# A vision tower on one core: query, key and value products from halves in fp16, and eleven more products of ones at the start

## What is computed

```python
h = embed(x, W, b)                      # patches of 768 numbers to 256
h = concatenate([cls_tok, h])           # 37 tokens per image
# attention on the normalized tokens, 4 heads of 64 channels
q, k, v = (split(norm(h) @ w.T) for w in (Wq, Wk, Wv))
p = softmax(causal(q @ k.T))
A_mem = (elu(q) + 1) @ mem / ((elu(q) + 1) @ z + 1e-6)
out = (g * A_mem + (1 - g) * (p @ v)) @ Wo.T + bo       # g = sigmoid(betas)
h = h + out
# one shared expert and the best 2 of 8 experts, hidden width 1024
h = h + shared(norm(h)) + sum(gate_e * expert_e(norm(h)) for e in top2(norm(h) @ gate_w.T))
```

## Time and profile before

| | |
|---|---|
| median of 3 executions | 331.41 us (331.07 to 331.76) |
| the profiled execution | 331.46 us |
| its span, first to last instruction | 329.6 us |
| busy share of the span | PE 96%, PEld 81%, DVE 67%, ACT 54%, POOL 43% |
| the chain that ended last | PE 77%, DVE 12%, issue 4%, DMA 3% |
| granted clock of TensorE, mean | 0.996 of full speed |

### The profile page before, as it was taken

How to read it: one execution, slowest core, us unless ns; L and a number is a source line. 1 busy time by engine, 2 the same in 40 slices (tenths; PEclk the granted TensorE clock), 3 DMA queues, 4 the chain that set the end, 5 groups by cost and what they waited for, 6 DMA issues and landing times.

```text
span 329.6 us, 9583 instructions
## 1 busy us (share of the span) xinstructions
PE 315.7 (96%) x3378; PEld 268.2 (81%) x3378; DVE 222.0 (67%) x501; ACT 177.3 (54%) x342; POOL 143.3 (43%) x216
## 2 busy tenths in 40 slices
PE   7999999999999899999999999999999999999990
PEld 6788888888888799999998777778777877777870
DVE  0336778888888888899887786855465655555540
ACT  1145667667786788557667877842323232323220
POOL 0566445555645432211451434555444453635131
PEclk9999999999999999999999999999999999999998
DMA  7775334332123113943689775332423232333221
GB/s 237 254 214 201 108 107 165 125 90 57 59 87 93 30 30 77 322 111 75 159 222 304 247 193 162 66 51 50 63 36 59 40 50 51 47 52 39 29 33 17
DMA packets 18641, 36.35 MB, mean 110 GB/s; under 512 B 3331, under 2 KB 10982, under 8 KB 18598
## 3 DMA queue, kind: packets, MB, share of 16 engines
q1 hardware_dynamic: 12166, 27.71, 26.5%
q0 software_dynamic: 6432, 8.03, 16.0%
HBM read 28.52 MB, written 7.21 MB: 108 GB/s over the span
## 4 chain that ended last, share of the span: by engine, by line
PE 77%; DVE 12%; issue 4%; DMA 3%; POOL 1%; ACT 1%; POOLq 1%; SPq 0%; DVEq 0%; ACTq 0%
PE bank L795 20%; PE bank L808 14%; PE bank L481 10%; PE bank L810 6%; PE bank L506 5%; PE bank L618 3%; PE bank L577 3%; PE bank L516 2%; DMA out_rows<-y,add_id 2%; PE bank L529 2%; PE bank L543 2%; PE bank L566 2%; DVE hid_lo L1339 2%; PE bank L436 2%; PE bank L533 1%
## 5 line engine op out<-in xcount | busy, mean ns | idle before, releaser
L795 PEld LDWEIGHTS bank<-x_t,weights 128*128 x1248 | 87.6, 98 | 25.6 <-issue 0.2
L795 PE MATMUL bank<-x_t,weights 128*128 128x128 f16 x1248 | 103.9, 219 | 0.0
L972 ACT ACTIVATE act_out<-bank 128x512 f32<-128x512 f32 (+2 forms) x72 | 42.0, 585 | 87.9 <-PE bank L795 75.4
L808 PE MATMUL bank<-weights,hid_hi 128*128 x192 | 73.3, 382 | 0.2
L1205 POOL DMA_INDIRECT out_rows<-y,add_id x26 | 42.1, 1618 | 70.6 <-DVE y L1540 52.3
L1339 DVE SCALAR_TENSOR_TENSOR hid_lo<-act_out,hid_hi 128x512 f16<-128x512 f32 (+2 forms) x72 | 48.6, 680 | 12.7 <-ACT hid_hi L983 11.2
L810 PE MATMUL bank<-weights,hid_lo 128*128 x192 | 52.3, 273 | 0.0
L1345 DVE SCALAR_TENSOR_TENSOR weights<-stage,weights 128x1024 f16<-128x1024 f32 x36 | 42.9, 1217 | 0.6 <-ACT weights L933 0.6
L933 ACT ACTIVATE weights<-stage 128x1024 f16<-128x1024 f32 x36 | 36.8, 1048 | 0.0
L481 PE MATMUL bank<-weights 128*111 128x256 f32 x132 | 33.0, 406 | 0.8 <-DMA weights<-in_w_embed 0.8
L1172 POOL DMA_INDIRECT slot_rows<-x_rows,gather_id x26 | 27.6, 1060 | 13.3 <-DMA out_rows<-y 5.5
(11 more groups left out here) (149 smaller groups left out, 530.9 us busy)
## 6 DMA issues: line engine op xcount, KB each, us to landing
stage<-in_w_ffn SPq DMA_DIRECT2D x36, 512.0 KB
weights<-in_patches SPq DMA_DIRECT2D x11, 333.0 KB, 3.7
x_rows<-rows SPq DMA_DIRECT2D x11, 111.0 KB
out_rows<-weights SPq DMA_DIRECT2D x10, 111.0 KB
out_rows<-y POOLq DMA_DIRECT2D x9, 119.0 KB, 6.1
weights<-in_w_embed SPq DMA_DIRECT2D x3, 256.0 KB, 3.8
weights<-in_w_qk SPq DMA_DIRECT2D x1, 512.0 KB, 5.9
slot_rows<-x_rows,gather_id POOLq DMA_INDIRECT x26, 3.7
```

What stands on the lines that cost most here:

```text
L795: mm = nc.tensor.matmul(o, weights[:, bass.ds(base + 2 * k * CHUNK + 2 * (col - col % D) + w * D + col % D, P)], x_t[:, b, (2 * x + k) * P ...
L808: nc.tensor.matmul(bank[5 + b][0:m, :], hid_hi[:, b, c * P:c * P + m], weights[:, bass.ds(at, 2 * D)], start=(c == 0), stop=False)
L972: nc.scalar.activation(d_, s_, ACT.Silu, scale=1.0 / (X_SCALE * W_SCALE)).then_inc(hid_acted, 1)
```

## The change

- The weights of query, key and value are loaded in the expert stages 4 and 5, multiplied by 64 and split in an fp16 high half by ACT (before its first norm) and a low half by DVE (`proj_lo_of`). SP waits for this before it loads chunks 4 and 5.
- `norm1` writes the normalized tile, now times 64, twice: in float32 and in fp16. The low half is their difference, `xln_lo`: on DVE for tiles 0, 1, 2 and 9, on POOL for the others. Both halves are turned by four fp16 transposes in place of two of float32, and ACT copies all four.
- `project_qk` issues 24 fp16 products in place of 8 of float32, `project_v` 6 in place of 2. ACT's copies of their results multiply by 1/4096.
- The channels within each head of query and key, and the rows of memory and z, stand in reverse order; the host does this.
- POOL makes the inverse deviations of both norms in one run of 8 operations on two columns (`inv_std_pair`) in steps 4 to 8, after the statistics of both. It also makes `row_lo` for tiles 0 to 4.
- The logits of tiles 0 to 4 stand in bank 1, where the turned tile stands too, and no longer in bank 6.
- PE turns the normalized tile ahead of `turn_rows` and `project_out`; the written list of the last tiles has `turn_rows(4)` and `logits(4)` one place on. ACT applies `norm2` after the exponentials, and copies the turned tile ahead of the turned rows. On DVE the preparation of gates and memory moves from the start of step 3 to step 2.
- `WARM` is 37 in place of 26.

The diff, cut to its core:

```diff
-WARM = 26
+WARM = 37
 RING = 7
 PATCH_RING = 3
 ROWS = 4
+POOL_ROWS = 5
+DVE_XLN = (0, 1, 2, NT - 2)
+PRODUCTS = ((0, 0, 0), (0, 0, 1), (0, 1, 0), (0, 1, 1), (1, 0, 0), (1, 0, 1))
...
+        qk_stage = stage[:, 4].rearrange("p (k d) -> p k d", k=KC)
+        v_stage = stage[:, 5, 0:KC * D].rearrange("p (k d) -> p k d", k=KC)
         slot_rows = sb("slot_rows", [P, 4, 2 * D], F16)
         x_t = sb("x_t", [P, 2, 4 * P], F16)
+        xln_pair = x_t
...
-        xln_t = part(2, KC, T)
+        xln_t = part(2 * KC * T).bitcast(F16).rearrange("p (r q t) -> p r q t", r=2, q=4)
...
+        def logits_in(t):
+            at = bank[1] if t <= NT - 7 else bank[6]
+            return at[0:T, D:D + 2 * EXPERTS]
...
+                elif c >= 4:
+                    sp.wait_ge(proj_lo, c - 3)
...
-            sp.dma_start(s_id, ident).then_inc(ident_in, 16)
+            sp.dma_start(id16[:], ident16).then_inc(ident_in, 16)
             load_patches(2)
-            sp.dma_start(s_wqk.rearrange("p a b c -> p (a b c)"), w_qk).then_inc(project_in, 16)
-            sp.dma_start(s_wv.rearrange("p a b -> p (a b)"), w_v).then_inc(project_in, 16)
+            sp.dma_start(stage[:, 4], w_qk).then_inc(w_qk_in, 16)
+            sp.dma_start(stage[:, 5, 0:KC * D], w_v).then_inc(w_v_in, 16)
...
             def turn_xln(t):
-                pe.wait_ge(xln_ready, t + 1)
+                pe.wait_ge(xln_lo_ready, t + 1)
                 if t == 0:
                     pe.wait_ge(ident_in, 16)
                     pe.wait_ge(h_ready, 2)
                 if t >= 1:
                     pe.wait_ge(xln_t_ready, t)
-                for k in range(KC):
-                    mm = nc.tensor.transpose(bank[1][:, k * T:(k + 1) * T],
-                                             xln[0:T, t % 2, k * P:(k + 1) * P], s_id[0:T, 0:T])
+                if t >= 6:
+                    pe.wait_ge(top_done, t - 5)
+                for q in range(4):
+                    mm = nc.tensor.transpose(bank[1][:].bitcast(F16)[:, q * 128:q * 128 + T],
+                                             xln_pair[0:T, t % 2, q * P:(q + 1) * P], id16[0:T, 0:T])
                 mm.then_inc(xln_turned, 1)
...
-                    pe.wait_ge(project_in, 2 * 16)
+                    pe.wait_ge(proj_lo, 1)
                 if t >= 1:
                     pe.wait_ge(qk_copied, t)
                 for o in range(4):
-                    for k in range(KC):
-                        mm = nc.tensor.matmul(bank[5][:, o * T:(o + 1) * T], s_wqk[:, k, o],
-                                              xln_t[:, t % 2, k], start=(k == 0), stop=(k == KC - 1))
+                    for n, (w, x, k) in enumerate(PRODUCTS):
+                        mm = nc.tensor.matmul(bank[5][:, o * T:(o + 1) * T],
+                                              w_qk16[:, k, w, o * P:(o + 1) * P],
+                                              xln_t[:, t % 2, 2 * x + k], start=(n == 0), stop=(n == 5))
                 mm.then_inc(qk_ready, 1)
 
             def project_v(t):
+                if t == 0:
+                    pe.wait_ge(proj_lo, 2)
                 if t >= 1:
                     pe.wait_ge(v_copied, t)
-                if t >= 5:
+                if t == NT - 1:
                     pe.wait_ge(top_done, t - 4)
-                for k in range(KC):
-                    mm = nc.tensor.matmul(bank[6][0:T, 0:D], xln_t[:, t % 2, k], s_wv[:, k],
-                                          start=(k == 0), stop=(k == KC - 1))
+                for n, (x, w, k) in enumerate(PRODUCTS):
+                    mm = nc.tensor.matmul(bank[6][0:T, 0:D], xln_t[:, t % 2, 2 * x + k], w_v16[:, k, w],
+                                          start=(n == 0), stop=(n == 5))
...
-                pe.wait_ge(v_copied, min(t + 5, NT))
+                if t <= NT - 7:
+                    pe.wait_ge(xln_t_ready, t + 6)
+                else:
+                    pe.wait_ge(v_copied, min(t + 5, NT))
                 if t >= 1:
                     pe.wait_ge(top_done, t)
-                both = bank[6][0:T, D:D + 2 * EXPERTS]
+                both = logits_in(t)
...
                     mix_values(s - 3)
+                if s == 0 or s >= 3:
+                    turn_xln(s)
                 if 0 <= s - 5:
                     turn_rows(s - 5)
                 if 0 <= s - 4:
                     project_out(s - 4)
-                if s == 0 or s >= 3:
-                    turn_xln(s)
...
-            turn_rows(s - 5)
             mix_values(s - 3)
...
             turn_prob(NT - 4)
+            turn_rows(NT - 7)
+            project_qk(NT - 2)
             logits(NT - 7)
-            project_qk(NT - 2)
...
+                if t >= 6:
+                    act.wait_ge(rstd2, t - 5)
                 if t >= 2:
                     act.wait_ge(xln_turned, t - 1)
-                nc.scalar.activation(xln[0:T, t % 2], h[0:T, t % RING], ACT.Identity,
-                                     scale=rstd[0:T, t % 2:t % 2 + 1],
-                                     bias=shift[0:T, t % 2:t % 2 + 1]).then_inc(xln_ready, 1)
+                at = slice(2 * (t % 2), 2 * (t % 2) + 1)
+                for dst in (xln[0:T, t % 2], xln_pair[0:T, t % 2, 0:D]):
+                    last = nc.scalar.activation(dst, h[0:T, t % RING], ACT.Identity, scale=rstd[0:T, at],
+                                                bias=shift[0:T, at])
+                last.then_inc(xln_ready, 1)
...
+            act.wait_ge(w_qk_in, 16)
+            nc.scalar.mul(w_qk16[:, :, 0], qk_stage, W_SCALE).then_inc(proj_hi, 1)
+            act.wait_ge(w_v_in, 16)
+            nc.scalar.mul(w_v16[:, :, 0], v_stage, W_SCALE).then_inc(proj_hi, 1)
...
-                if 0 <= s - 5 and s < NT - 1:
-                    norm2(s - 5)
                 if 0 <= s - 2:
                     exps(s - 2)
                 if s >= NT - 2:
                     copy_v(s - 1)
-                if s >= NT - 1:
+                if 0 <= s - 5:
                     norm2(s - 5)
                 if 0 <= s - 1:
                     tanh_q(s - 1)
-                if s == NT - 1:
+                if s < NT:
                     copy_xln_t(s)
                 if 0 <= s - 5:
                     copy_x2_t(s - 5)
-                if s < NT - 1:
-                    copy_xln_t(s)
...
+            def inv_std_pair(t1, t2):
+                pool.wait_ge(stats1, t1 + 1)
+                pool.wait_ge(stats2, t2 + 1)
+                at = slice(2 * (t1 % 2), 2 * (t1 % 2) + 2)
+                v_, y_, z_, n_ = var_eps[0:T, at], newton[0:T, 0, at], newton[0:T, 1, at], newton[0:T, 2, at]
+                link(nc.gpsimd.tensor_scalar_add(v_, mv[0:T, at, 1], EPS))
+                link(nc.gpsimd.tensor_tensor(y_, v_, half[0:T], ALU.pow))
+                link(nc.gpsimd.tensor_tensor(z_, y_, y_, ALU.mult))
+                link(nc.gpsimd.tensor_tensor(z_, z_, v_, ALU.mult))
+                link(nc.gpsimd.tensor_scalar(z_, z_, 0.5 * X_SCALE, -1.5 * X_SCALE, ALU.mult, ALU.add))
+                link(nc.gpsimd.tensor_tensor(n_, z_, y_, ALU.mult))
+                nc.gpsimd.tensor_tensor(shift[0:T, at], n_, mv[0:T, at, 0], ALU.mult).then_inc(rstd1, 1)
+                nc.gpsimd.tensor_scalar(rstd[0:T, at], n_, -1.0, None, ALU.mult).then_inc(rstd2, 1)
...
+            def xln_lo(t):
+                pool.wait_ge(xln_ready, t + 1)
+                pool.wait_ge(xln_lo_ready, t)
+                nc.gpsimd.tensor_tensor(xln_pair[0:T, t % 2, D:], xln[0:T, t % 2], xln_pair[0:T, t % 2, 0:D],
+                                        ALU.subtract).then_inc(xln_lo_ready, 1)
+            def row_lo(t):
+                pool.wait_ge(row_hi_ready, t + 1)
+                nc.gpsimd.tensor_tensor(rows[0:T, t % ROWS, D:2 * D], xln2[0:T, t % 2],
+                                        rows[0:T, t % ROWS, 0:D], ALU.subtract).then_inc(row_lo_ready, 1)
...
+                    if s not in DVE_XLN:
+                        xln_lo(s)
                     pool.wait_ge(xln_ready, s + 1)
                     nc.gpsimd.tensor_tensor(h[0:T, s % RING], h[0:T, s % RING], s_ob[0:T],
                                             ALU.add).then_inc(h_bo_ready, 1)
+                if 0 <= s - 5 < POOL_ROWS:
+                    row_lo(s - 5)
                 if 0 <= s - 1 < NT:
                     relu_q(s - 1)
-                if s + 2 < NT:
-                    inv_std(s + 2, stats1, rstd1, s % 2, 1.0)
-                if 0 <= s - 4 < NT - 2:
-                    inv_std(s - 4, stats2, rstd2, 2 + s % 2, X_SCALE)
+                if s < 4:
+                    inv_std(s + 2, stats1, rstd1, 2 * (s % 2))
+                if 0 <= s - 4 and s + 2 < NT:
+                    inv_std_pair(s + 2, s - 4)
...
+            def proj_lo_of(n, dst, src):
+                dve.wait_ge(proj_hi, n + 1)
+                nc.vector.scalar_tensor_tensor(out=dst[:, :, 1], in0=src, scalar=W_SCALE, in1=dst[:, :, 0],
```

(38 more changed lines are left out.)

96 lines of the change are left out of this document (45 added, 51 removed).

## The result

| | before | after |
|---|---|---|
| median of 5 executions, run side by side | 331.75 us (331.07 to 332.15) | 326.19 us (325.89 to 326.52) |
| ratio | | 0.9842, interval [0.9824, 0.986] |
| the profiled execution, its span | 331.46, 329.6 | 325.89, 324.0 |

The change makes the kernel faster by 1.6%, and the forecast of 325.4 us was 0.8 too low. The sum inside it was less good than that. For the start and steps 1 to 3 it had 1.6 us of gain too much, for the steady steps 0.9 too little, and that the two partly cancel is luck. Most of what follows is about that.

A forecast was written before the change was run, and what follows sets the result against it. PE was taken to bound the pipelined front, at 9.60 us a step. Start 0.3, steps 1 to 3 1.55, steady steps 3.1, then 0.7 - 0.2 + 0.65 sum to 6.1: 331.46 to 325.4 us, range 322.0 to 328.0.

The forecast's parts named there:

- The products: On PE, per tile: query and key 1.92 to 1.27 us, value 0.87 to 0.66, together 0.86 gained.
- Start: Up to the query and key products of tile 0: a gain of 0.3 us (-0.5 to +0.4).
- Steps 1 to 3: Early front: PE's gain, not all passed on, less 0.19 for a longer copy: 1.55 us.
- QK(3) to QK(8): Five steady steps: 5 x 0.86, plus 0.2 for an earlier turn, less 1.4 for blocked POOL: 3.1 us.
- the loop of 8.0: Steady steps: statistics, inverse-deviation pair, POOL's wide operations, row turn, projection, next residual: 8.0 us (7.5 to 8.9), under 8.74.
- Steps 9 and 10: End of the front: 0.7 of DVE's wait for the mix goes, 0.2 lost to xln_lo(10) on POOL.
- QK(10): Query and key products of tile 10: the chain passes through them to scores(9), 0.65 us gained.
- (a): Rival, steady steps: POOL's operations miss DVE's split, the 1.4 isn't given back: 324.0 us; chance 0.23.
- (b): Rival, steps 5 to 8: POOL's loop binds at about 9.6 us, 1.06 gained for 3.1: 327.4; chance 0.20 with (e).
- (c): Rival, steady steps: POOL's loop meets a full block twice a step, 11.3 us: 334.2, slower; chance 0.06.
- (d): Rival, after the front: the DVE stage to 157 us absorbs the gain: 331.4 us; chance 0.05.
- (e): Rival, PE: fp16 products pass no faster than 0.08 us each, 24 take 1.92: 328.8; chance 0.20 with (b).

The follow-up runs named there:

- no_split: The changed kernel with zeros written by DVE memsets in place of the low halves of query, key and value weights: 325.35 us, ratio 0.9819.
- split_in_quarters: The changed kernel with every weight split of DVE in the front made in pieces of 256 columns: 326.49 us, ratio 0.9839.
- rows_on_dve: The changed kernel with row_lo back on DVE for all tiles, ahead of the weight split: 331.99 us, ratio 1.0023.
- v_split_late: The changed kernel with the split of the value weights moved behind the embedding's residual of tile 2: 326.62 us, ratio 0.984.
- warm26: The changed kernel with 26 products of ones in place of 37: 326.73 us, ratio 0.986.

## Why the prediction was right, and where it wasn't

**The products.** Right. 1.92 to 1.23 or 1.25 and 0.87 to 0.66, as the row of 24 products of 119 columns said. The Trainium skill's rule of four passes ("FP8 and Floating Point Precision", TensorE Precision Notes) gives 0.48 for the first gain; the trace doesn't agree, it is 0.67 to 0.69. For the value product the rule gives 0.22, and the trace agrees with 0.21.

**Start, 0.3 forecast, -0.04 measured.** The step that failed is the path to the low half of tile 0. It was built from w_v's landing, ACT's 0.55 and the norm, and so ended at 15.1. Two instructions of the change itself were left out of it. ACT's split of the query and key weights starts when w_qk lands, at 11.31, and so the norm came at 12.79 and not at 12.5. And DVE's own split of 1.22 stands ahead of `xln_lo(0)`, from 12.98 on; `no_split` puts 0.21 on it. The path that the traces show instead begins with the patches of tile 1 and runs through DVE's queue (residual and statistics of tile 1, split, low half), 6.49 us from their landing to QK(0). The part on the clock was right (the ones end at 4.31, even before the forecast's 4.7), and worthless in this kernel, since the patches came no earlier than 9.08 here and 8.62 in any trace. With another landing the measured -0.04 would be anything from -0.2 to +0.4.

**Steps 1 to 3, 1.55 forecast, 0.26 measured.** The prediction knew that POOL's small operations stand still beside a split of DVE, and charged it to the steady steps, where splits had always been. It didn't ask the same of the two new splits. They fall on the inverse deviation of tile 1, for which ACT, DVE and PE all wait in turn. `no_split` gives 1.36 us back at tile 1, of which 0.21 was lost at tile 0 already, and `split_in_quarters` 0.49.

**QK(3) to QK(8), 3.1 forecast, 3.98 measured.** 5 x 0.86 + 0.2 fits, and the 1.4 for the blocked POOL was the term that was mis-sized: the periods exceed 8.74 only by 0.38 and 0.11 where they exceed it, some 0.5 in all. A block there is as long as expected, but in three of the four steps it falls on the last of the pair's operations, when next to no one waits. In the step from 62.43 the pair begins 1.12 after its start (forecast 1.35), the split 3.87 (4.55), and the row's low half ends at 7.09 (7.93), where PE takes it up at 7.15 (7.6 by the forecast). The timeline of after, in the one step where it is on the path, from tile 4 to tile 5:

```profile
48.20 1.36 POOL L1173 TENSOR_TENSOR weights<-weights 111x2 f32<-111x2 f32 x1
48.29 1.22 DVE L1423 SCALAR_TENSOR_TENSOR weights<-stage,weights 128x1024 f16<-128x1024 f32 x1
...
50.08 0.60 ACT L987 ACTIVATE weights<-weights 111x256 f32<-111x256 f32 x1 [0.58 <-POOL weights L1175]
...
51.33 0.63 POOL L1202 TENSOR_TENSOR rows<-weights,rows 111x256 f16<-111x256 f32 x1
...
52.01 0.37 PE L513 MATMUL bank<-id,rows 111*128 111x111 f16 x4 [0.23 <-POOL rows L1202]
```

and its groups of the step from 61.50 to 70.20 (busy us, mean ns, idle before), which answer to the earlier trace rows:

```profile
L1175 POOL TENSOR_SCALAR weights<-weights 111x2 f32<-111x2 f32 x1 | 1.5, 1532 | 0.0
...
L1202 POOL TENSOR_TENSOR rows<-weights,rows 111x256 f16<-111x256 f32 x1 | 0.6, 630 | 0.0
L1173 POOL TENSOR_TENSOR weights<-weights 111x2 f32<-111x2 f32 x1 | 0.3, 344 | 0.1
...
L1170 POOL TENSOR_TENSOR weights<-weights 111x2 f32<-111x2 f32 x1 | 0.2, 198 | 0.1
```

The small tensor_tensor was taken as 0.36 and takes 0.20 in three of four cases, and the row's low half 0.63 in place of 0.72. The one pair that no block touches takes 2.8 us (81.12 to 83.90; forecast 3.3, bounds 2.8 to 4.2), and by the same sum the loop of 8.0 is about 7.4, an estimate from these rows. That is the slack in which most of the blocks vanish.

**Steps 9 and 10, and QK(10).** 0.7 - 0.2 = 0.5 forecast, 0.46 measured. DVE's first instruction behind the mix, at 91.40 before, stands at 86.71. That is 4.69 earlier, 0.49 more than QK(8), where the term was 0.7. Its wait is still 0.72, since the mix now stands behind the turn of tile 9, and DVE's low half for that turn met a POOL operation and took 0.98 in place of 0.42. The forecast had no such price there:

```profile
83.86 0.72 POOL L1218 TENSOR_TENSOR weights<-weights 111x256 f32<-111x256 f32 x1
83.87 0.98 DVE L1366 TENSOR_TENSOR x_t<-weights,x_t 111x256 f16<-111x256 f32 x1
...
86.71 0.16 DVE L1329 TENSOR_SCALAR weights<-bank 111x4 f32<-111x4 f32 x1 [0.72 <-PE bank L555]
```

From there to QK(10) 0.03 is lost, where the term was 0.2. In six of the other traces some 0.6 is lost to the meeting of DVE and POOL at 92 us. QK(10) 0.65 forecast; from tile 10 (4.66) to the expert stage (5.29) it is 0.63.

**The rivals.** (a), POOL misses the split, is refuted as to its reason (it is hit, 1.53 us in the step above) and nearer than the forecast as to its price in the steady steps (0.5, between 0 and 1.4). (b), a loop of 9.6, isn't there: the periods are 8.4 to 9.1. (c) would have needed a loop of 10.6; a loop of 10.2 does appear in `rows_on_dve`, by a wait at the head of DVE's queue that the prediction hadn't named. (d) didn't come: 4.66 at tile 10 is 5.6 at the end of the span. (e) is refuted by the 1.23.

## What to carry to other kernels

When work is taken from the engine that sets the pace, ask at each stage of the pipeline whether it sets the pace there: here the same edit was worth 0.8 us a tile in the steady steps and 0.2 in all over the first three. Every new wide two-input operation on DVE is also a block of POOL, so charge it at every place where it is added, by what POOL is doing then. Before two traces are compared, look for the first event that no edit touches (here the landing of a transfer) and count from it: a gain of 0.3 us in `v_split_late` was such a landing and nothing else. And when one instruction moves on an engine (the second norm behind the exponentials), check each reader that stands ahead of its new producers on another queue: a place off by a few instructions cost 5.3 us.

## What the runs showed of the hardware

- The block between DVE and POOL goes both ways. Beside a split of 1.22 us POOL's operations on 111 x 1 or 111 x 2 took 1.12 to 1.75 us in after, in place of 0.2 to 0.6; beside a POOL operation of 0.72, DVE's two-input ones took 0.98 in place of 0.39 and 0.42. The Trainium skill ("SBUF — State Buffer", Who interferes with whom, Practical consequences) has the exclusion for whole instructions, by order of issue. The lengths agree. The order can't be read from the profile's starts: at 91.96 and 91.97 (v_split_late) DVE's stands first and DVE waits, at 92.28 and 92.31 (after) it stands first and POOL waits. And four DVE instructions in a row without a gap held POOL through all four (1.75) or let it in between them (0.32, 0.61), as told under `split_in_quarters`.
- A wide single-input POOL operation is held up too: `relu_q` takes 0.98 alone and 2.02 beside a split, in the timeline of after:

```profile
32.41 1.21 DVE L1423 SCALAR_TENSOR_TENSOR weights<-stage,weights 128x1024 f16<-128x1024 f32 x1
32.45 2.02 POOL L1189 TENSOR_SCALAR weights<-weights 128x222 f32<-128x222 f32 x1
```

- Behind 26 products of ones and an idle stretch of 0.82 us, the embedding's first instructions last 634 ns each in the median (before and warm26); behind 37, which end at 4.31 in after, 379 ns. The granted clock of the profile reads 1.00, its 2.4 GHz level, from 4.40 to 9.00 us in both. The patches behind them landed between 8.62 and 9.37 in all traces in which the embedding waited for them.
